# Two transformer layers with cross-attention on one core: chunk 0's keys stored earlier, two steps of the first batch reordered, last token tile summed on TensorE

## The reference

```python
x = x + _L0_xattn_ref(_layernorm(x), ctx_1024, ...)      # rotary, bias, gate
x = x + _L0_ffn_ref(_layernorm(x), ...)                  # tanh(x W A1 A2 + b)
x = x + _L1_xattn_ref(_layernorm(x), ctx_1024, ctx_1024, mask, ...)
x = x + _L1_ffn_ref(_layernorm(x), ...)
# the last line, per token:
y = jnp.einsum('bsd,edf->bsef', x, expert_W) + expert_b
out = jnp.einsum('bsef,bse->bsf', y, comb) / K           # comb: 2 of 8 weights, K = 2
```

## Time and profile before

| what | us |
|---|---|
| median of 3 runs | 569.89 |
| lowest and highest | 567.97, 572.94 |
| the profiled execution, its own time | 571.24 |
| its span, first to last instruction | 567.8 |
| PE busy | 505.2 (89%) |
| ACT busy | 433.0 (76%) |
| DVE busy | 280.4 (49%) |
| POOL busy | 171.2 (30%) |

### The profile page before, as it was taken

The page is one execution under the profiler, slowest core; times in us unless marked ns, Lnnn a source line. Parts: engine busy times, 40 slices in busy tenths (PEclk is TensorE's granted clock), DMA queues, the critical chain, the costliest instruction groups (busy, mean ns, idle before and its releaser), DMA issues.

```text
span 567.8 us, 15324 instructions
## 1 busy us (share of the span) xinstructions
PE 505.2 (89%) x6318; PEld 256.2 (45%) x6318; DVE 280.4 (49%) x741; ACT 433.0 (76%) x493; POOL 171.2 (30%) x207
## 2 busy tenths in 40 slices
PE   7677798899889998999999999899989999998994
PEld 4344454445444554455555444444444444343332
DVE  4853665774586455654523252325434543261156
ACT  1235587677768787687898999899988998899841
POOL 4464945486488124871001000100000000000003
PEclk9897999999999999999999999999999999999998
DMA  8575884579557802575184356229411840000000
GB/s 264 157 231 161 258 289 112 158 223 306 142 161 214 304 16 75 166 218 163 27 178 141 110 123 158 60 46 202 119 55 47 178 145 2 12 1 1 8 6 15
DMA packets 51583, 74.52 MB, mean 131 GB/s; under 512 B 11146, under 2 KB 40050, under 8 KB 51506
## 3 DMA queue, kind: packets, MB, share of 16 engines
q1 hardware_dynamic: 40258, 37.54, 26.4%
q0 software_dynamic: 5632, 24.07, 12.9%
q10 hardware_dynamic: 5616, 11.86, 6.7%
HBM read 39.95 MB, written 18.83 MB: 104 GB/s over the span
## 4 chain that ended last, share of the span: by engine, by line
PE 60%; ACT 15%; issue 10%; DVE 8%; POOL 4%; DMA 2%; ACTq 0%; DVEq 0%; POOLq 0%
PE ps L538 26%; PE ps L514 16%; ACT probs L1173 9%; PE ps L449 4%; PE ps L439 2%; PE ps L668 2%; ACT ctx_turned L1173 2%; DVE k_swapped L1473 1%; PE ps L443 1%; ACT ctx_tokens L1173 1%; DMA k_scratch<-k_parts 1%; ACT k_parts L1198 1%; PE ps L702 1%; PE ps L550 1%; PE ps L519 1%
## 5 line engine op out<-in xcount | busy, mean ns | idle before, releaser
L1173 ACT ACTIVATE probs<-ps 124x1024 f32<-124x1024 f32 (+1 forms) x305 | 296.2, 1025 | 56.1 <-PE ps L519 44.6
L514 PE MATMUL ps<-q_side,k_side 64*124 64x256 bf16 (+1 forms) x1664 | 161.9, 290 | 38.3 <-ACT probs L1173 30.1
L538 PE MATMUL ps<-probs,values 124*9 124x256 f32 (+1 forms) x2440 | 162.8, 382 | 0.0
L514 PEld LDWEIGHTS ps<-q_side,k_side 64*124 64x124 bf16 (+1 forms) x1664 | 79.4, 130 | 144.9 <-ACT probs L1173 77.4
L538 PEld LDWEIGHTS ps<-probs,values 124*9 124x9 f32 (+1 forms) x2440 | 52.7, 90 | 63.5 <-issue 16.7
L1043 POOL TENSOR_TENSOR post_rstd<-post_rstd,power 128x2 f32<-128x2 f32 x12 | 8.4, 703 | 194.2 <-DVE post_rstd L1688 126.7
L519 PE MATMUL ps<-bias_near,bias_w 64*124 64x84 bf16 (+1 forms) x416 | 42.2, 200 | 0.0
L1173 ACT ACTIVATE ctx_tokens<-ps 124x1024 f32<-124x1024 f32 (+1 forms) x37 | 38.0, 1026 | 4.9 <-PE ps L514 4.0
L1473 DVE SCALAR_TENSOR_TENSOR k_swapped<-ps,beta_products,k_table_sb 32x496 f32<-32x496 f32 (+2 forms) x64 | 40.4, 632 | 0.9
L1173 ACT ACTIVATE ctx_turned<-ps 124x1024 f32<-124x1024 f32 (+1 forms) x37 | 37.9, 1025 | 3.4 <-PE ps L514 2.4
L1173 ACT ACTIVATE ctx_normed<-ps 124x1024 f32<-124x1024 f32 (+1 forms) x37 | 37.9, 1025 | 2.4 <-PE ps L514 1.6
(11 more groups left out here) (250 smaller groups left out, 634.7 us busy)
## 6 DMA issues: line engine op xcount, KB each, us to landing
k_side<-k_scratch SPq DMA_DIRECT2D x24, 400.2 KB, 7.8
k_scratch<-k_parts POOLq DMA_DIRECT2D x16, 372.0 KB, 4.9
k_side<-k_parts SPq DMA_DIRECT2D x45, 124.0 KB, 2.4
q_side<-q_parts SPq DMA_DIRECT2D x63, 64.0 KB, 2.5
v_scratch<-values POOLq DMA_DIRECT2D x4, 936.0 KB, 9.9
values<-v_scratch SPq DMA_DIRECT2D x4, 936.0 KB, 14.3
v_scratch<-v POOLq DMA_DIRECT2D x12, 288.0 KB, 4.7
mask_q<-in_mask POOLq DMA_DIRECT2D x8, 400.5 KB, 4.2
```

Of the source, the lines that this page charges most:

```text
L514: last = pe.matmul(ps[0:width, bank, SQ * i:SQ * (i + 1)], kst[rows, j % 2, 2 * g + i, at], qst[rows, query_slot(j, run), 2 * g + i, :], s ...
L538: last = pe.matmul(ps[32 * i:32 * i + VC, ACC + g // 2, SQ * (g % 2):SQ * (g % 2) + SQ], v[0:rows, j % 2, t, h, :], probs_of(u)[0:rows, SQ ...
L1173: act.activation(probs_of(u)[0:rows, :], ps[0:rows, s:s + 2, :].rearrange("p a n -> p (a n)"), ACT.Exp)\
```

## The change

It has four parts.

1. POOL stores chunk 0's keys right behind the parts of chunk 1, ahead of the ones and of the wait for unit 4. Chunk 1's stores stay behind that wait.
2. In the first batch DVE does `norm_queries(0)` between the values and the middle part of chunk 3, and PE's `centre_x` fills HIGH before LOW.
3. At the end DVE does the token statistics before the finiteness check and its minimum. ACT takes over the second copy of the sums and the copy of tile 0 of y.
4. Tile 1 is summed on PE in one PSUM region: x, the expert biases, and the eight products that ACT has scaled, each through a 128x128 identity. ACT copies the result out. POOL's `add_last` goes.

```diff
+SCALED_LAST = (0, 1, 4, 5, 2, 3, 6, 7)
...
             def centre_x(k):
                 pe.wait_ge(xrest_in, 16)
+                fill(HIGH, "xn", k)
+                spread_x(HIGH, 0, range(NB * k, NB * k + NB), 0).then_inc(made[HIGH], 1)
                 fill(LOW, "xn", k)
                 pe.matmul(ps[:, LOW, :], centre[:], x[:, 512 * k:512 * k + 512], start=True, stop=True).then_inc(made[LOW], 1)
-                fill(HIGH, "xn", k)
-                spread_x(HIGH, 0, range(NB * k, NB * k + NB), 0).then_inc(made[HIGH], 1)
...
             pe.transpose(ps[0:1, HIGH, 0:128], least[:], ident[:]).then_inc(made[HIGH], 1)
+            last_tokens = slice(NT - D, NT)
+            pe.matmul(ps[:, ACC, 0:D], x[:, last_tokens], ident[:], start=True, stop=False, skip_group_check=True)
             for k in (2, 3):
                 experts(NB - 1, k)
+            pe.matmul(ps[:, ACC, 0:D], comb_t[:, 128 * (TT - 1):128 * TT], eb[:], start=False, stop=False, skip_group_check=True)
+            for i, e in enumerate(SCALED_LAST):
+                pe.wait_ge(last_scaled, i + 1)
+                last = pe.matmul(ps[:, ACC, 0:D], ident[:], p[:, 0, D * e:D * e + D], start=False, stop=i == E - 1, skip_group_check=True)
+            last.then_inc(last_added, 1)
...
             second_parts(1)
+            store_keys(0, 0)
             ones_of_values(1)
             pool.wait_ge(scores_ready, 5)
-            for n in range(2):
-                store_keys(0, n)
+            store_keys(0, 1)
             parts(0, 2)
...
             redo_of["POOL"] = read_redo(pool)
-            add_last()
...
+            act.wait_ge(probs_used, UB * NJ)
+            act.wait_ge(made[HIGH], side.of(HIGH, "pick", NJ - 2))
+            act.activation(oacc[:, 512:1024], ps[:, ACC + 1, :], ACT.Copy).then_inc(sums_copied, 1)
+            act.wait_ge(made[HIGH], side.of(HIGH, "xt", NB - 1))
+            act.wait_ge(e_aggr, TT * NB)
+            act.wait_ge(out_sem, 16 * TT * (NB - 2))
+            act.activation(y[:, (NB - 1) % 2, 0, :], ps[:, HIGH, 0:128], ACT.Copy).then_inc(seen[HIGH], 1)
             act.wait_ge(gate_step, GATE_STEPS * (NB - 1) + 3)
...
+            act.wait_ge(last_added, 1)
+            act.activation(y[:, (NB - 1) % 2, TT - 1, :], ps[:, ACC, 0:D], ACT.Copy).then_inc(y_done[TT - 1], 1)
...
-                for n in range(2):
+                for n in range(2 if j < NJ - 1 else 1):
...
+                if b == NB - 1:
+                    return
                 if b > 1:
                     dve.wait_ge(out_sem, 16 * TT * (b - 1))
...
-            keys(0, 3)
-            for k in range(2):
-                norm_queries(k)
-                turn_queries(k)
+            rotate_keys(0, 3)
+            both_values(0, 3, 0)
+            high_part(0, 3)
+            both_values(0, 3, 1)
+            norm_queries(0)
+            middle_part(0, 3)
+            turn_queries(0)
+            norm_queries(1)
+            turn_queries(1)
...
             project(NB - 1)
+            token_norm(NB - 1)
             check_finite(NJ - 1)
             least_of_checks()
-            token_norm(NB - 1)
             choose_last()
```

More of the change, by code:

```diff
@@ L1058, in rank_last @@
                 pool.tensor_tensor(ecmp[:], ecmp[:], etie[:], ALU.add).then_inc(rank_step, 1)
[L1060 to L1071, removed]
             def ones_of_values(slot):
@@ L1325, in scalar_program @@
             act.wait_ge(comb_r_ready, 1)
-            for i, e in enumerate((0, 1, 4, 5, 2, 3, 6, 7)):
+            for i, e in enumerate(SCALED_LAST):
                 if i == 2:
@@ L1815, in add_bias @@
                 dve.wait_ge(made[LOW], side.of(LOW, "base", b))
-                dve.tensor_tensor(out, out, ps[:, LOW, 0:SQ].rearrange("p (t d) -> p t d", d=D), ALU.add).then_inc(seen[LOW], 1)
+                n = TT if b < NB - 1 else 1
+                dve.tensor_tensor(out[:, 0:n], out[:, 0:n], ps[:, LOW, 0:D * n].rearrange("p (t d) -> p t d", d=D), ALU.add)\
+                   .then_inc(seen[LOW], 1)
                 dve.wait_ge(seen[LOW], side.of(LOW, "base", b))
```

## The result

| what | us |
|---|---|
| kernel after, median of 9 runs | 565.37 (564.50 to 566.26) |
| kernel before beside it, median of 9 runs | 570.91 (567.97 to 572.94) |
| ratio | 0.9908, 95% interval 0.9888 to 0.9927 |
| profiled execution after, its span | 565.75, 564.2 |

The change gains 0.92%, some 5.3 us by the ratio (5.5 by the medians). That is faster beyond doubt, but within the 1% for which the prediction gave 0.14, not the gain of over 1% for which it gave 0.83. The forecast was 561.3; 565.37 lies at the very end of the range (565.4). Compared with the forecast's own frame, the profiled execution went from 571.24 to 565.75: 5.49 us in place of 8.6.

A forecast was written before the change was run, and what follows sets the result against it. The prediction took the run as mostly matmul-bound on PE, with a store wait delaying the first batch. Its terms, 5.0 + 2.55 + 0.8 + 0.45 - 0.2 = 8.6 us, gave 561.3 us against the median; range 558.8 to 565.4.

The forecast's parts named there:

- The store: Chunk 0's keys stored earlier: `second_keys(0, 2)` moves from 43.37 to 38.35, gaining 5.0 us.
- The clock: Unit 7's scores to unit 9's values: PE's shorter gap keeps its clock at full, gaining 2.55 us.
- The context rows: Batch 1's 832 KB load behind `second_keys`: lands before DVE wants it, charged nothing, up to 2 us in the bound.
- rival C: Context rows meet the backlog and land too late, delaying chunk 3: slower than before, 573.2 us; chance 0.03.
- the first order: First batch, `norm_queries(0)` ahead of DVE's cast: line 413 starts earlier, gaining 0.8 us.
- Part 2: First batch's two reorderings: 0.8 us at the queries, 0.45 us at the second centring.
- The end: Last tile summed on PE instead of POOL: 0.2 us slower, bounds 0.7 gained and 1.1 lost.
- A: First batch: late rows, a slow third store or a clock dip absorb 2 to 3 us; about 563.5 us; chance 0.23.
- B: At `second_keys`: third store lands in 8.7 us, PE still idles and loses its clock; 567.6 us; chance 0.12.
- D: First batch gains as forecast and PE holds full clock at the end; 560.4 us; chance 0.62 together with the forecast.

The follow-up runs named there:

- e12: Kernel after with the load of x's second part (384 KB) moved behind the context rows; 562.65 us, ratio 0.9888.
- second repeat: Kernel before, unchanged, profiled once more in a single run; 568.22 us.
- e7: Kernel after with 12 matmuls of zeros on PE ahead of unit 7's scores; 563.17 us, ratio 0.9893.
- e1: Kernel before with only the early store of chunk 0's keys; 565.73 us, ratio 0.9927.
- e4: Kernel after with POOL's `add_last` put back for tile 1; 564.30 us, ratio 0.9900.
- e6: Kernel after with the store that `second_keys` waits for issued first of chunk 0's three; 564.32 us, ratio 0.9922.
- e10: e6 with batch 1's context rows issued earlier, behind unit 4's exponential, and x's second part in their old place; 560.53 us, ratio 0.9853.
- e2: Kernel before with only the two reorderings of the first batch; 568.34 us, ratio 0.9966.
- e5: Kernel after with nine matmuls of zeros on PE ahead of the last tile's gathers; 563.90 us, ratio 0.9901.
- e3: Kernel before with only the changes at the end (parts 3 and 4); 570.11 us, ratio 1.0013.
- e13: e10 with nine matmuls of zeros on PE ahead of the last gathers; 560.39 us, ratio 0.9850.

## Why the prediction was wrong

**The store: 5.0 forecast, 4.3 measured.** The mechanism, the place and nearly the size were right: `second_keys` was to start at 38.35 and starts at 38.58. That it came so near is in part luck: the landing was put at 5.0, "near the transfer's own row", and took 6.0, but the store was issued 0.8 sooner than forecast. The reason given for less than 5.9, the share of 0.43 in 32 to 34, looked at the wrong stretch: the packets travel in 34 to 38, at a share of 0.97 and more, most of it other queues' loads: POOL's queue has 10 to 13% of the engines there, the queue of the loads 86 to 90%. e12 shows the crowding, with 4.4. Ahead of the second centring, where the profile of the kernel before has the engines at 0.21 to 0.71, the same store for the next batch took 3.2:

```profile
94.00:96.00 2.00, 2.00 (x28) 1.39 (x28) 0.76 (x2) 0.82 (x2) 2.00 (x4) 1.00 0.71 165
...
k_scratch<-k_parts POOLq DMA_DIRECT2D x1, 93.0 KB, 3.2
```

The Trainium skill, "DMA: Bandwidth & Descriptors", section "Anatomy of one DMA — SWDGE (gpsimd) path", fits 2.0 us plus the bytes over its rate, by an estimate 2.2 us for 93 KB; no store of keys came that low here, the least in any profile being 2.4.

**The clock: 2.55 forecast, 0.03 measured.** This is the step that failed: "With PE's gap cut from 6.23 to some 1.3 us I expect the clock to hold". The gap was 3.33. It is the difference of two arrivals, PE's and ACT's, and only ACT's had been worked out. PE's arrival was taken over from a profile in which PE was itself late: line 449's eight products ran at the low clock there, 3.67 us, and unit 0 began at 31.25. The prediction quoted that row, for the price of a pass, and did not ask whether it would be so again. In the kernel after unit 0 begins 1.95 us earlier. PE is out of work at 40.79 - 3.33 = 37.46 in place of 45.58 - 6.23 = 39.35, so 1.9 of the 2.1 us by which the gap is longer than forecast are PE's, and 0.2 ACT's. In the kernel before an early PE costs nothing: with unit 0 at 28.72 (second repeat) the gap is 6.17, since the stores wait for unit 4 and come earlier with it. Part 1 takes that wait away, and so also what kept the two arrivals together. The size of the term was right: e7, which only fills the gap, has 3.11 for the steps and 2.5 us less up to the queries. The 0.03 is that of one pair of profiles; in e1 and e4 about 1 and 1.3 us of the term came.

**The context rows: charged at nothing.** True of the kernel after (DVE waits for nothing at 49.58), and so rival C is wrong for it. But only because the clock had already taken the gain. e6 shows what the forecast would have met: wanted 15.6 us after unit 0 (the prediction: 46.8 - 31.25 = 15.55), there at 19.1. "they took 5.5 with the old backlog, so I charge nothing" failed; issued into full engines they took 10.9. Store, clock and the first order were to bring 8.35 us at the first product of the queries. The kernel after has 37.49 - 33.77 = 3.7 of it, e6 5.5, and e10, which moves the rows too, 8.1, with a time of 560.53. The forecast's 561.3 thus belongs to a kernel with two more edits, the awaited store issued first and the two loads exchanged.

**Part 2: 0.8 and 0.45 forecast, 0.85 and 0.74 measured**, and 1.9 us by e2 (0.7 to 3.1). The first is the wait of 0.79 that is gone. Of the second, 0.46 is line 472's wait (0.87 to 0.41), as forecast; the other 0.28 lies elsewhere between the two points and has no cause shown. The cast was to be "late by some tenths"; behind `norm_queries` it starts at 63.03 and even runs in 0.41 us in place of 1.31; POOL is between two steps for that time, where before it was at work for most of the cast.

**The end: 0.2 slower forecast, 1.57 in the last step of the profile, 0.9 from the second centring to the end.** The price of a pass was right at either level (0.13 and 0.23 forecast; 2.05 / 16 = 0.128 in e5 and 3.78 / 16 = 0.236 after). The choice of a value between them was wrong: in both profiles of the kernel after the clock was at the low level. It can go the other way: with the gathers the last step took 4.23 and 4.22 there, 2.70 in e3 and 2.46 in e6. By medians (e3 against before, e4 against after) nothing to 1 us. The Trainium skill, "TensorE: Matmul & The Clock Gate", section "Part 1: The HAM clock gate (the "warmup" mystery)", lets an idle array run at 1.2 GHz; the trace of the kernel after agrees, with 0.50 in 556 to 558 behind a PE without work in 552 to 554, and e5, with zeros in that place, keeps 1.00.

**The rivals.** What happened is A's mixture near its lower end: "the third store takes 6 to 7 us, or the clock dips", 8.6 - 3 = 5.6 against 5.49. It had a chance of 0.23, too little for a case that names three separate mishaps, of which any one is enough. Its other mishap, rows that come late, waited just behind. B's place and its lost clock were right, its size (a landing of 8.7) wrong. C and D did not come.

## What to carry to other kernels

A gap is two arrivals: when a wait is shortened, look up for both engines how they vary between executions, the waiting one too, before counting on a clock that holds. A store moved into a burst of loads lands by what is queued around it in the stretch where its packets travel, so move the awaited one to the front (5.6 to 6.0 us became 3.8 and 4.6) or bulk loads away (4.4; with both, 3.4 to 4.2). And before the gain of an earlier stage is booked, find the next transfer with a fixed place: here 832 KB of rows that nobody had awaited, until a stage came 4.8 us early, took three of them back. When two transfers change places, which of the two moves paid needs a run of its own.

## What was not expected of the hardware

- The landing of one store of 93 KB, of the same line, lay between 2.7 and 7.0 us by its place and its execution, that of the 832 KB of rows between 5.0 and 11.1.
- Ahead of unit 7, PE's clock held behind idle gaps of 1.01 and 1.50 us (e6, e10 and e13) and fell behind 1.81 (e12) and, in every profile, behind 2.92 and more. It cost 1.2 to 2.6 us (4.36 to 5.73 against 3.11), not in the order of the gaps.
- Twelve zero matmuls in a gap of 3.3 us cost nothing that shows and kept the clock (e7). At the end of the kernel they made the last step 2.4 us shorter in the profile, of which the median showed 1 at most.
- In three profiles of the kernel before the products ahead of unit 0 took 1.99, 2.70 and 3.67 us, and unit 0 started at 28.72, 30.43 and 31.25.
